# The first convolution of a graph-network kernel by three half-rate products instead of seventeen direct taps

## The reference

```python
h = relu(layernorm(x))
x = x + L0(h, adj)
h = relu(layernorm(x))
x = x + adj @ (h @ weight) + bias
# L0, per graph
x_conv = relu(bn2(conv1d(relu(bn1(conv1x1(h))), 17 taps, pad 8)) + h)   # along the nodes
s = h @ w_se.T + b_se;  A = exp(-|s_n - s_m|^2) * adj
x_nmp = A @ relu(h @ w_msg.T + b_msg)
return GRU(input = [x_conv, x_nmp], hidden = h)
```

## Time and profile before

| | |
|---|---|
| median of 3 runs | 347.7 us (345.97 to 348.69) |
| profiled execution | 345.98 us, its span 344.1 us |
| PE busy | 331.1 us (96%) |
| DVE, ACT, POOL busy | 263.2, 220.8, 151.7 us |
| step 0 until `step(1)` begins on PE | 0 to 68.04 us |

### The profile page before, as it was taken

One profiled execution on the slowest core, in us unless ns is written; L12 is line 12 of the kernel. 1 busy time (PEld: TensorE's weight loads), 2 busy tenths in 40 slices (PEclk: granted clock), 3 DMA queues, 4 the chain that ended last, 5 costly groups with the idle time before them and its releaser, 6 DMA issues.

```text
span 344.1 us, 6334 instructions
## 1 busy us (share of the span) xinstructions
PE 331.1 (96%) x2212; PEld 297.5 (86%) x2212; DVE 263.2 (76%) x735; ACT 220.8 (64%) x431; POOL 151.7 (44%) x131
## 2 busy tenths in 40 slices
PE   8699979999999999999999999999999999999995
PEld 5489968799989998899989998899989998899884
DVE  5597987898688976898688977898677968674473
ACT  2958745977775785667775785667776655452443
POOL 7053370035932297035922297036920396055014
PEclk9999999999999999999999999999999999999999
DMA  7900100001310031001210031001100000001001
GB/s 233 339 4 0 61 33 0 2 1 53 102 33 1 3 122 63 0 0 59 99 31 0 4 123 61 0 2 61 65 0 2 0 32 30 3 0 63 0 1 64
DMA packets 7952, 15.04 MB, mean 44 GB/s; under 512 B 1008, under 2 KB 1648, under 8 KB 7792
## 3 DMA queue, kind: packets, MB, share of 16 engines
q1 hardware_dynamic: 7776, 14.62, 12.4%
q10 hardware_dynamic: 144, 0.01, 0.0%
HBM read 10.43 MB, written 4.19 MB: 43 GB/s over the span
## 4 chain that ended last, share of the span: by engine, by line
issue 41%; POOL 30%; PE 13%; DVE 9%; ACT 5%; DMA 1%; POOLq 1%; DVEq 0%; ACTq 0%
POOL x_ring L1350 5%; POOL base L1362 3%; POOL rs L1297 3%; POOL ac L940 3%; POOL px L944 2%; POOL px L934 2%; POOL px L937 2%; POOL base L1365 2%; POOL rs L1302 2%; POOL base L1356 2%; DMA vec<-vec_in 1%; PE pNR L305 1%; PE pNR L303 1%; PE pNR L304 1%; ACT conv_hi L658 1%
## 5 line engine op out<-in xcount | busy, mean ns | idle before, releaser
L1302 POOL TENSOR_TENSOR rs<-ve,neg_half 128x4 f32<-128x4 f32 x15 | 15.6, 1039 | 94.7 <-DVE ve L1086 94.7
L1297 POOL TENSOR_TENSOR rs<-ve,neg_half 128x8 f32<-128x8 f32 (+1 forms) x9 | 15.5, 1720 | 73.0 <-DVE ve L964 73.0
L303 PE MATMUL pP<-cx_hi,conv_hi 128*128 128x256 f32 x154 | 45.1, 293 | 0.0
L305 PE MATMUL pP<-cx_hi,conv_lo 128*128 128x256 f32 x154 | 43.5, 282 | 0.0
L304 PE MATMUL pP<-cx_lo,conv_hi 128*128 128x256 f32 x154 | 43.3, 281 | 0.0
L303 PE MATMUL pQ<-cx_hi,conv_hi 128*128 128x256 f32 x126 | 37.2, 295 | 0.0
L305 PE MATMUL pQ<-cx_hi,conv_lo 128*128 128x256 f32 x126 | 35.4, 281 | 0.0
L304 PE MATMUL pQ<-cx_lo,conv_hi 128*128 128x256 f32 x126 | 35.4, 281 | 0.0
L732 ACT ACTIVATE work<-work,nb,rs 128x128 f32<-128x128 f32 x60 | 24.8, 483 | 15.1 <-DVE nb L1090 15.1
L303 PEld LDWEIGHTS pP<-cx_hi,conv_hi 128*128 128x128 f32 x154 | 29.1, 189 | 0.3
L304 PEld LDWEIGHTS pP<-cx_lo,conv_hi 128*128 128x128 f32 x154 | 29.1, 189 | 0.3
(11 more groups left out here) (275 smaller groups left out, 1071.7 us busy)
## 6 DMA issues: line engine op xcount, KB each, us to landing
x_ring<-x_in SPq DMA_DIRECT2D x16, 256.0 KB, 2.8
adj_ring<-adj_in SPq DMA_DIRECT2D x16, 256.0 KB, 3.0
out<-x_ring SPq DMA_DIRECT2D x15, 256.0 KB, 2.0
work<-conv_in SPq DMA_DIRECT2D x1, 1088.0 KB, 8.0
x_ring<-gate_in SPq DMA_DIRECT2D x1, 576.0 KB, 7.6
out<-x_ring SPq DMA_DIRECT2D x2, 128.0 KB, 1.8
early<-early_in SPq DMA_DIRECT2D x1, 129.5 KB, 3.4
late<-late_in SPq DMA_DIRECT2D x1, 128.0 KB, 7.9
```

The costliest lines, as they stand in the source:

```text
L303: pe.matmul(acc, w_hi, m_hi, start=start, stop=False)
L305: return pe.matmul(acc, w_lo, m_hi, start=False, stop=stop)
L1297: pool.tensor_tensor(rs1[:, lane], ve1[:, lane], neg_half[:, lane], ALU.pow).then_inc(rs1_set, 1)
L1302: pool.tensor_tensor(rs2[g % 2][:], ve2[g % 2][:], neg_half[:, 0:GG], ALU.pow).then_inc(rs2_set, 1)
```

## The change

Only step 0 is changed, and what the engines do around it. Its convolution becomes a two-way fast one: three products, each of 8 taps at half rate, `even_tap` on differences (even phases less odd phases) into `pQ`, `sum_tap` (even plus odd taps, on the odd phases) into `pP`, `odd_tap` on other differences into `pP` again. Both outputs need the second product, so DVE adds it to both residuals (`with_sum`) before the third may overwrite `pP`. Tap 16 is added to `pQ` and `pP` once each. The sums of taps move from POOL (`sum_phases`) to DVE (`sum_odd`, `sum_halves`), the differences for step 0 are made by DVE (`less_odd`, `next_less_odd`), and the four-way differences for step 1 on POOL all wait for the fourth `pair_rows`.

```diff
-        W_PARTS = (taps(8, A0), taps(8, A2), taps(1, T16), taps(4, M22), taps(8, M12), taps(8, M21))
+        W_PARTS = (taps(4, A0), taps(4, A2), taps(1, T16), taps(8, M21), None, taps(4, M22), taps(8, M12))
...
-        FIRST_ORDER = (0, 3, 4, 1, 2)
+        FIRST_ORDER = (0, 3, 1, 4, 2)
...
+            def half_rate(bank, part, w, j, start=False, stop=False):
+                x = FIRST_AT[part]
+                if j % 2 == 0:
+                    parts = [(bank[:], slice(x, x + 2), j // 2)]
+                else:
+                    parts = [(bank[:, 0:CG * QN], slice(x + 1, x + 2), j // 2),
+                             (bank[:, CG * QN:], slice(x, x + 1), j // 2 + 1)]
+                for acc, phases, at in parts:
+                    last = split_product(acc, w_hi, w_lo, cx_hi[:, phases, :, at * GG:at * GG + QW],
+                                         cx_lo[:, phases, :, at * GG:at * GG + QW], start, stop)
...
@@ PE, opening
                 pe.wait_ge(w_split, 1)
+                pe.wait_ge(cxlo_set, 1)
+                even_tap(0)
+                even_tap(2)
+                even_tap(4)
+                even_tap(6)
+                messages(1)
...
+                even_tap(7).then_inc(f_done[0], 1)
+                pe.wait_ge(w_split, 4)
                 pe.wait_ge(cxlo_set, 2)
...
+                half_rate(pQ, 2, T16, 8, stop=True).then_inc(f_done[3], 1)
...
+                pe.wait_ge(w_split, 5)
+                pe.wait_ge(cxlo_set, 4)
+                pe.wait_ge(t0_set, 2)
+                odd_tap(0)
...
+                half_rate(pP, 1, T16, 8, stop=True).then_inc(f_done[4], 1)
                 gates_h(0)
...
@@ DVE
+            def less_odd():
+                dve.wait_ge(c1_set, 2)
+                dve.tensor_tensor(px[:, 0:2], c1[:, 0:2], c1[:, 2:4], ALU.subtract).then_inc(diff_set, 1)
+            def sum_odd():  # 128 x 1024
+            def sum_halves():  # 128 x 1024, then 128 x 512
+            def with_sum(e):
+                dve.wait_ge(f_done[1], 1)
+                dve.scalar_tensor_tensor(base[e][:], phases(1), bn_a[:, 1:2], base[e][:], ALU.mult, ALU.add).then_inc(t0_set, 1)
...
@@ POOL, opening
-                pool.wait_ge(cxlo_set, 2)
                 scale1([2, 3])
-                sum_phases()
-                pre(pool, 1, 1)
-                pre(pool, 1, 2)
                 pool.wait_ge(pair_set, 4)
-                for k in range(3, 6):
+                for k in range(1, 6):
                     pre(pool, 1, k)
                 scale1([4, 5])
```

More of the change, by code:

```diff
@@ L313, in product, with even_tap, sum_tap, odd_tap @@
                 return last
-            def direct(tap, start=False, stop=False):
-                w = T16 if tap == 16 else 4 * (tap % 4) + tap // 4
+            def half_rate(bank, part, w, j, start=False, stop=False):
                 w_hi, w_lo = conv_hi[:, w * D:(w + 1) * D], conv_lo[:, w * D:(w + 1) * D]
[L318 to L332, removed]
+                x = FIRST_AT[part]
[7 more added lines that the diff above has]
+                                         cx_lo[:, phases, :, at * GG:at * GG + QW], start, stop)
+                return last
+            def even_tap(j):
+                return half_rate(pQ, 0, (A0, A2)[j % 2] + j // 2, j, start=j == 0)
+            def sum_tap(j):
+                return half_rate(pP, 1, (M21, M23)[j % 2] + j // 2, j, start=j == 0, stop=j == 6)
+            def odd_tap(j):
+                return half_rate(pP, 3, (A1, A3)[j % 2] + j // 2, j, start=j == 0)
             def four(first, more=False):
@@ L514, in opening @@
+                sum_tap(3)
+                conv1(2)
                 distances(0)
-                pe.wait_ge(w_split, 2)
-                direct(2)
-                conv1(2)
+                x_turn(3)
+                sum_tap(5)
                 distances(1)
                 messages(2)
-                x_turn(3)
-                direct(6)
+                sum_tap(7)
                 neighbour_sums(0)
-                direct(10)
+                sum_tap(6).then_inc(f_done[1], 1)
+                pe.wait_ge(cxlo_set, 3)
@@ L532, in opening @@
-                rows_turn(3)
-                direct(11)
+                odd_tap(6)
                 distances(3)
+                odd_tap(1)
+                odd_tap(3)
                 neighbour_sums(2)
[L536 to L542, removed]
+                odd_tap(5)
@@ L670, in hidden_graphs @@
                 have(act, hT_placed, g + 1)
[L671 removed]
+                have(act, hlo_set, g + 1 if g < 4 else 0)
                 act.activation(hn[g % 2][:].rearrange("p (g n) -> p g n", g=GG),
@@ L931, in pre @@
                 have(eng, pre_set, pre_before(t) + 3)
-            have(eng, cxlo_set, cx_before(t) if t > 1 else 0)
+            have(eng, cxlo_set, cx_before(t))
             if k == 1:
@@ L1152, in opening @@
                 normalise1([2, 3])
+                sum_odd()
+                coordinates(1)
+                split_lo_first(1)
                 split_w(2)
+                split_w(3)
+                shift1([2, 3])
                 pair_rows(0)
-                coordinates(1)
-                shift1([2, 3])
                 pair_rows(1)
+                hidden_lo(2)
                 right_rows(0)
-                hidden_lo(2)
+                next_less_odd()
                 right_rows(1)
+                split_lo_first(2)
                 masked(0)
-                split_w(3)
+                hidden_lo(3)
                 coordinates(2)
+                masked(1)
                 split_w(4)
-                hidden_lo(3)
-                masked(1)
                 pair_rows(2)
+                split_lo_first(3)
+                with_sum(0)
+                with_sum(1)
                 sums_lo(0)
-                dve.wait_ge(gate_rounded, 1)
-                dve.tensor_tensor(gate_lo[:], gate, gate_hi[:].bitcast(F32), ALU.subtract).then_inc(gate_split, 1)
-                split_w(5)
                 coordinates(3)
@@ L1177, in opening @@
                 right_rows(3)
-                normalise1([4, 5])
+                conv_out(0, 0)
+                split_lo(1, 0)
                 masked(3)
+                dve.wait_ge(gate_rounded, 1)
+                dve.tensor_tensor(gate_lo[:], gate, gate_hi[:].bitcast(F32), ALU.subtract).then_inc(gate_split, 1)
                 sums_lo(2)
-                conv_out(0, 0)
-                shift1([4, 5])
-                split_lo(1, 0)
                 conv_lo_out(0, 0)
+                split_lo(1, 3)
+                split_lo(1, 1)
+                sum_halves()
                 conv_out(0, 1)
-                split_lo(1, 3)
                 conv_lo_out(0, 1)
                 sums_lo(3)
+                normalise1([4, 5])
+                split_w(5)
+                shift1([4, 5])
+                split_w(6)
+                blend_start(0)
+                blend_end(0)
                 split_lo(1, 4)
-                blend_start(0)
-                split_lo(1, 1)
                 split_lo(1, 2)
-                blend_end(0)
                 hidden_lo(4)
```

167 lines of the change are left out of this document (96 added, 71 removed).

## The result

The changed kernel takes **349.65 us** (median of 15 runs, 348.59 to 350.4), the kernel before 347.7 (15 runs, 345.97 to 349.3). The ratio is 1.0041, 95% interval 1.0024 to 1.0057: a little slower and clear of noise. By the medians the change costs 1.95 us, by the ratio 1.4 us; forecast were 3.8 (351.5). The profiled execution took 348.94 us, its span 347.1.

The account below looks back on a forecast made before the run. PE was taken as the bound, busy 331 of 344 us. A lag of 1.4 us plus 2.4 for a clock fall made +3.8, on the median 347.7 giving 351.5 us; range 347.1 to 353.0.

Parts of the forecast that it names:

- Work removed, 5.6 us: PE in step 0: 26 units of three passes instead of 34, 0.23 us per pass, so 5.6 us less.
- The start at 15.8: PE's convolution in step 0 starts at 15.8 instead of 17.04 us, 1.2 us earlier.
- DVE's stretched operations gone: DVE's 2.36 and 2.44 us operations, held up by POOL, should vanish; some 6 to 7 us given back.
- The five pauses in the middle (0.4, 1.0, 1.3, 1.3, 1.45): PE waits at the first `sum_tap`, `x_turn(2)`, the first `odd_tap`, `rows_turn(3)` and `distances(3)`, in us.
- The pause ahead of `x_turn(4)`: PE stands still 5.5 to 6 us for `first(4)`, behind late `normalise1([4, 5])`; `x_turn(4)` at 64.1 instead of 62.26.
- Without the clock +2.0 us: Whole kernel: the 4.7 us lead becomes a lag, 2.0 us slower if the clock stays up.
- what PE wins by `step(1)` is carried to the end: Steps 1 to 7 are dense PE work, so PE's gain or loss by `step(1)` at 68.04 us stays.
- The clock falls in the pause: At the restart at 64.1, 4.9 us at half speed lose 2.4 us; this forecast's chance 0.40.
- The sum: Whole kernel: 1.4 lag + 2.4 clock = +3.8 us, added to the median 347.7, gives 351.5.
- the lower bound is nothing: Clock's price after a pause: pauses of 2.1 and 2.0 us were followed by full clock, so possibly no loss.
- rival 1: The pause before `x_turn(4)` is there but the clock stays up: +2.0, 349.7 us; chance 0.27.

Follow-up runs that it names:

- gate_early: Changed kernel with the gate weights' rounding (ACT) and split (DVE) moved to earlier rows, statistics of groups 4 and 5 left in place: 349.59 us, ratio to before 1.0047.
- first_ahead: Changed kernel with two ACT rows exchanged, `first(4)` ahead of `candidate(0)`: 346.48 us, ratio to before 0.9967.
- stats_early: gate_early with `normalise1([4, 5])` and `shift1([4, 5])` on DVE and `first(4)` on ACT moved earlier: 343.56 us, ratio to before 0.989.
- pause_filled: Changed kernel with 24 idle PE products ahead of `x_turn(4)`, in its long pause: 348.0 us, ratio to before 1.0004.
- before_fill_two: Kernel before with 15 instead of 6 idle products ahead of its convolution and 8 before `distances(3)`, filling both pauses: 346.15 us, ratio to before 0.9943.
- control: Kernel before, without an edit, run against itself: 348.47 us, ratio 1.0023.
- combined: stats_early with `shift1([2, 3])` ahead of `split_w(3)` and `right_rows(3)` ahead of `masked(2)` on DVE: 343.69 us.

## Why the prediction was wrong

- **Work removed, 5.6 us: right.** The six groups of 25 records of the direct convolution are three of 25 and three of 13, 36 instructions fewer. Counted by width they are 26 units of three passes instead of 34.
- **The start at 15.8: right** (15.88). **DVE's stretched operations gone: right.** The shift of 128x8 takes 0.16 us instead of 2.36, the split of 1024 takes 1.22 instead of 2.44, and DVE's busy time is 264.1 us against 263.2.
- **The five pauses in the middle (0.4, 1.0, 1.3, 1.3, 1.45): right in kind, mostly a little large.** Measured: 0.1 (22.50 to 22.64), 0.79, 0.63, 1.03, 1.58. `gates_h(0)` at 48.70, forecast "48 to 49".
- **The pause ahead of `x_turn(4)`: right.** Forecast at 64.1 after 5.5 to 6 us; measured 64.51 after 6.07. gate_early, first_ahead and stats_early show the mechanism: less work on DVE brings nothing, one exchanged row on ACT 3.2 us, earlier statistics 6.1. Both figures hold the clock's 1.65 us; against pause_filled they are 1.5 and 4.4.
- **Without the clock +2.0 us: right.** pause_filled less before_fill_two, both without a fall of the clock, is 348.0 - 346.15 = 1.85 us (2.1 by their ratios to before, 1.0004 and 0.9943). That what PE wins by `step(1)` is carried to the end is not right for an earlier start: first_ahead begins it 0.9 us before the old time and ends 0.6 us later.
- **The clock falls in the pause: right; its price of 2.4 us was too large.** I took the 4.9 us of the program's start, from one execution. There half speed was read from the pace of the products alone, as the granted clock reads 1.00 in this stretch; in pause_filled the sixteen products from 5.09 on take 1.97 us instead of 2.63, so its slow stretch is 3.6 us at most. Behind the pause the half-speed work lasted 3.2 us, and filling the pause brings 1.65 us.
- **The sum: here it failed.** The step that failed is the clock's term: 2.4 us, added in full to the median of before. I wrote "the lower bound is nothing" for pauses of 2 us, from one profiled execution, and then added the clock's full price to the *median* of before. That median already held falls of its own: 347.7 against 346.15 with both pauses filled, 1.55 us. The change removes the first of these pauses (2.1 us becomes 1.0) and shortens the second to 1.6, and pays one fall in the long pause instead, by the mean clocks in every run. Split up by the filled kernels, the changed one is 346.15 + 1.85 + 1.65 = 349.65 and before 346.15 + 1.55 = 347.7. The clock's part of the change is 1.65 - 1.55 = 0.1 us, not 2.4. By the ratios to before it is 1.3 - 2.0, or -0.7 us (the 1.0041 of the changed kernel less the 1.0004 of pause_filled, and 1 less the 0.9943 of before_fill_two), and 2.1 us without the clock. Either way it is near nothing or below.

Between the two profiled executions the difference is 3.0 us, nearer to my 3.8: against an execution of before that had no fall, as 7 of the 29 have. The sum with the price measured at `step(1)` would have been 1.4 + 1.5 = 2.9 there, so between two executions with a known clock the walk holds. I had noted that the median stood 1.7 us above the profiled execution and didn't ask what it was; 1.6 us is one fall of the clock.

So rival 1 gave the right number, 349.7, by luck: it has the clock stay up. The clock does fall, but it did before as well, and the two nearly cancel.

## What to carry to other kernels

A change that saves work on the bounding engine has to be followed to the next instruction that this engine can't start: here 5.6 us of removed passes were lost, above all to statistics that came late on DVE and to a row of ACT that stood behind a late blend. Before a cost is added to a median, the spread of the runs has to be explained; levels at equal distances with their own mean clock are a second cost that the profiled execution may lack. Filling both pauses of the kernel before with idle products made it 1.5 us faster and took most of its spread (0.5 instead of 3.5 us).

## What the runs showed that I had not expected

- The clock can fall 1.2 us after the work has begun again (control: PE back at 17.0, half speed from 18.2 to 21.6), behind a pause of 2.1 us, and in other executions of the same program not at all. The Trainium skill (TensorE: Matmul & The Clock Gate, "What's actually happening") describes a window that runs on its own and doesn't start with the kernel; the differing executions agree with that.
- The clock fell behind short waits too. In the profiled execution of stats_early it is half from about 11.8 to 15.2 us. Since PE's first products its longest wait was one of 0.82 us, ending at 11.76; waits of 0.36, 0.51 and 0.16 us stand between 7 and 10 us:

```profile
11.00:11.50 0.50, 0.00 (x0) 0.00 (x0) 0.49 (x1) 0.50 (x2) 0.00 (x0) 1.00 1.02 408
11.50:12.00 0.50, 0.24 (x1) 0.25 (x2) 0.20 (x1) 0.50 (x2) 0.00 (x0) 0.83 0.98 388
12.00:12.50 0.50, 0.50 (x2) 0.40 (x3) 0.00 (x0) 0.50 (x1) 0.00 (x0) 0.50 1.05 411
```

- A fall has no fixed price: about 1.6 us each in the kernel before, 0.7 in stats_early, 0.1 to 0.4 in combined. Where PE meets waits for DVE or ACT later on, as in `step(1)` of first_ahead, lost time of PE can be covered by them; that this is the reason is argued, not shown.
- In first_ahead, with a pause of 3.0 us, some executions have a mean clock of 1.00 and some of 0.995, and all lie within 346.28 to 346.67: there the fall seems to cost next to nothing. Where it lay in those executions no trace shows.
- POOL is held up as well: its power of 128x8 takes 1.65 us alone and 2.01 beside the split of DVE that starts at 57.32.
